# Another order of the pieces of a step in the five engines' queues of a Mamba and mixture-of-experts kernel

## What is computed

```
h = causal_conv(x_hat @ in_proj, 4 taps) + conv_b         # u
dt = clip(sigmoid(u @ dt_w.T + dt_b), 1e-4, 1);  Bm, Cm = u @ B_w.T, u @ C_w.T
state = exp(dt*A) * state + dt*Bm*u + 1e-6                # for each of 16 states, along 256 tokens
y = sum_n(state_n * Cm_n) + D*u;   x = x + (y * silu(z)) @ out_w.T
w = normalised top 2 of sigmoid(x_hat @ router_w.T + bias)
x = x + shared(x_hat) + sum_e w_e * (silu(x_hat @ wg_e.T) * (x_hat @ wu_e.T)) @ wd_e.T
```

## Time and profile before

| | |
|---|---|
| median of the runs | 1398.56 us (1398.08 to 1398.73) |
| the profiled execution: its span | 1397.1 us (its own time is this span and the launch around it, some 1.5 us by the median) |
| TensorE matmuls busy | 1212.7 us, 87% |
| VectorE busy | 1174.3 us, 84% |
| ScalarE busy | 916.8 us, 66% |
| GpSimd busy | 846.8 us, 61% |
| the chain that ended last | TensorE 35%, VectorE 31%, ScalarE 13%, issue 12%, GpSimd 5%, DMA 2% |
| mean granted TensorE clock | 0.981 of 2.4 GHz |

### The profile page before, as it was taken

How to read it: one execution, slowest core, us unless ns; L and a number is a source line. 1 busy time by engine, 2 the same in 40 slices (tenths; PEclk the granted TensorE clock), 3 DMA queues, 4 the chain that set the end, 5 groups by cost and what they waited for, 6 DMA issues and landing times.

```text
span 1397.1 us, 27129 instructions
## 1 busy us (share of the span) xinstructions
PE 1212.7 (87%) x8709; PEld 1013.2 (73%) x8709; DVE 1174.3 (84%) x2236; ACT 916.8 (66%) x1464; POOL 846.8 (61%) x1370
## 2 busy tenths in 40 slices
PE   6878897899989898998989899898989989898883
PEld 4556666577877777777777778777877878787773
DVE  1699999998898979998898989989798988998423
ACT  4665666577875766777676777668577768772321
POOL 4445445854366864768656783768647684665554
PEclk9899999999999999999999999999999999999997
DMA  6000000032322343143321433232330333256783
GB/s 179 1 1 9 1 9 6 22 125 61 114 82 64 106 136 103 44 128 99 121 67 34 147 97 98 86 111 81 109 120 29 125 92 121 78 184 190 251 271 85
DMA packets 111646, 132.29 MB, mean 95 GB/s; under 512 B 10128, under 2 KB 82704, under 8 KB 111504
## 3 DMA queue, kind: packets, MB, share of 16 engines
q1 hardware_dynamic: 98416, 111.31, 25.7%
q0 software_dynamic: 8192, 16.79, 4.0%
q10 hardware_dynamic: 4896, 2.43, 0.6%
HBM read 102.37 MB, written 28.11 MB: 93 GB/s over the span
## 4 chain that ended last, share of the span: by engine, by line
PE 35%; DVE 31%; ACT 13%; issue 12%; POOL 5%; DMA 2%; DVEq 0%; POOLq 0%; SPq 0%; ACTq 0%
DVE h L1281 14%; DVE yT L1299 11%; PE p_db L1036 5%; PE p_misc L1060 5%; PE p_hT L1053 5%; PE p_dn L1218 4%; PE p_gu L1206 3%; ACT dA L872 3%; ACT L969 2%; POOL ysel L791 2%; ACT hm L969 2%; PE p_gu L1197 2%; PE p_misc L1097 2%; PE p_misc L1141 1%; PE p_misc L1115 1%
## 5 line engine op out<-in xcount | busy, mean ns | idle before, releaser
L1281 DVE TENSOR_TENSOR_SCAN h<-dA,p_db 128x512 f32<-128x512 f32 x512 | 602.4, 1205 | 86.3 <-PE p_db L1036 85.3
L735 POOL TENSOR_SCALAR dBT<-wT,bcT 128x256 f32<-128x256 f32 x704 | 337.1, 479 | 249.2 <-ACT wT L903 140.1
L1299 DVE SCALAR_TENSOR_TENSOR yT<-p_hT,bcT,yT 128x256 f32<-128x256 f32 x960 | 402.2, 472 | 18.0 <-PE p_hT L1053 17.9
L872 ACT ACTIVATE dA<-dt_sb,A_sb 128x510 f32<-128x510 f32 x512 | 330.6, 710 | 26.6 <-DVE h L1281 25.5
L1036 PE MATMUL p_db<-ident,dBT 128*128 128x128 f32 x2048 | 284.4, 277 | 49.4 <-DVE h L1281 44.0
L1053 PE MATMUL p_hT<-ident,h 128*128 128x128 f32 x2048 | 288.9, 279 | 29.8 <-DVE yT L1299 16.6
L1036 PEld LDWEIGHTS p_db<-ident,dBT 128*128 128x128 f32 x2048 | 233.4, 142 | 96.7 <-issue 84.7
L1053 PEld LDWEIGHTS p_hT<-ident,h 128*128 128x128 f32 x2048 | 233.0, 143 | 74.8 <-issue 42.2
L777 POOL DMA_INDIRECT xs_dram<-xn,slot x128 | 127.0, 992 | 90.0 <-ACT dA L872 38.3
L929 ACT ACTIVATE dBT<-wT,eps,bcT 128x256 f32<-128x256 f32 x320 | 163.9, 593 | 0.0
L791 POOL DMA_INDIRECT ysel<-ys_dram,slot x128 | 123.5, 965 | 57.0 <-issue 33.9
(11 more groups left out here) (189 smaller groups left out, 1533.1 us busy)
## 6 DMA issues: line engine op xcount, KB each, us to landing
wring<-w_moe_dram SPq DMA_DIRECT2D x169, 384.0 KB, 4.3
xt<-xs_dram SPq DMA_DIRECT2D x41, 256.0 KB, 5.7
ys_dram<-yo SPq DMA_DIRECT2D x34, 256.0 KB, 2.3
dA<-w_moe_dram SPq DMA_DIRECT2D x16, 384.0 KB, 5.6
x_sb<-x_dram SPq DMA_DIRECT2D x16, 256.0 KB, 4.5
out_dram<-x SPq DMA_DIRECT2D x15, 256.0 KB, 2.5
xs_dram<-ysel SPq DMA_DIRECT2D x4, 512.0 KB, 6.0
xs_dram<-xn,slot POOLq DMA_INDIRECT x128, 2.3
```

The lines of the kernel that those rows point to most:

```text
L735: op = pool.tensor_scalar(dBT[:, j % DBT_RING, c], wT[:, g % 2, c], bcT[:, g % 2, c, n:n + 1], STATE_EPS, ALU.mult, ALU.add)
L872: act.activation(dst[:, :, 1:], src[:, :, 1:], ACT.Exp, scale=A_sb[:, half, n:n + 1]).then_inc(exp_done, 1)
L1281: dve.tensor_tensor_scan(h[:, j % 2, half], dA[:, j % DA_RING, half], p_db[half][:], 0.0, ALU.mult, ALU.add).then_inc(scan_done, 1)
L1299: op = dve.scalar_tensor_tensor(yT[:, g % 2, cc], p_hT[pair][:, c], bcT[:, g % 2, cc, NS + n:NS + n + 1], yT[:, g % 2, cc], ALU.mult, ALU.add)
```

## The change

In the last steps, of group 15's routing `r`: before `r0` to `r25` in a row after `lg`; after `lg r0-3 P P r4-12 P P r13-22 Q P P r23-25`. GpSimd: before `S S C S S C S...`, after `C C S S S S S...` (combs of group 11, scatters of the last batch, then gathers). The diff, cut to the tables spoken of:

```diff
 PE_SLOTS = (
-    "U h N G i0 i1 X", "h U yb0 N i0 i1 yb1 G", "X h U xnT i0 i1 N G", "h u0 N U v0 i0 i1 X X",
-    "N h U G op i0 i1", "U X G h u1 v1 G N i0 i1 h", "U X xn2T G i0 i1 dt0 f0 X",
-    "N h dt1 f1 N U i0 i1 logit X G", "h N U i0 i1 G bc N X", "h U i0 i1", "h G G N X U z0 i0 i1 z1",
-    "h X N U G i0 i1 X U rank", "N h i0 i1", "h G X wT0 U N wT1 G i0 i1 h X N X", "U G N i0 i1 h G",
-    "U i0 i1 X")
+    "X U i0 U N h N G i1", "h yb0 G i0 i1 h G N yb1", "i0 N i1 U U xnT h u0 i0", "G i1 v0 N X h op X U",
+    "i0 G X i1 h u1 v1 G X", "N U i0 i1 X U xn2T G h", "i0 dt0 N f0 i1 X N h i0", "dt1 f1 U i1 G logit h U X",
+    "i0 i1 X bc h X N i0 N", "i1 U h i0 G N z0 G X", "i1 h G U N i0 z1 G i1", "X U i0 h rank U N h i1",
+    "N wT0 X U G G wT1 i0 X", "N h i1 U i0 G i1 h X", "X U N i0 i1 G")
 DVE_SLOTS = (
-    "stats1 s0 s1 y0 P y1", "C Q s0 s1 Q P yd0 y0", "s0 s1 yd1 y1 Q C y0 y1", "s0 C C y0 s1 P y1 P Q",
-    "s0 s1 P y0 y1 x1 C", "stats2 s0 s1 C y0 Q Q P y1", "s0 s1 y0 P y1", "s0 y0 s1 C Q y1 s0 lg P Q",
-    "s1 Q C y0 P C", "s0 y1 s1 r y0 r y1 r P r r s0 r", "Q C s1 r y0 y1 r P r Q r s0 s1 r",
-    "r y0 r P y1 r C C Q r", "s0 r s1 r y0 y1 r r", "C P r r s0 s1 Q r y0 y1 r Q r",
-    "r r C s0 P s1 r r y0 r P y1", "s0 C s1 C Q y0 Q P y1")
+    "s0 stats1 P s1 y0 y1 C P s0 s1", "Q yd0 s0 s1 C y0 yd1 y1 Q C", "y0 y1 s0 s1 y0 P y1 P s0 Q",
+    "s1 y0 y1 Q Q x1 stats2 P s0 s1", "C y0 C y1 s0 P P s1 C Q", "y0 y1 s0 s1 C y0 y1 s0 P s1",
+    "Q lg Q y0 r y1 r P s0 r", "s1 Q r y0 y1 r P s0 r s1", "C Q r y0 C r y1 r Q s0", "r P C s1 r y0 r C y1 s0",
+    "r s1 r Q P C r C r y0", "r y1 r P r y0 r Q r s0", "s1 r y1 Q P r s0 r y0 r", "Q y1 r C s1 r s0 r P C",
+    "s1 y0 Q y1 C P r")
 ACT_SLOTS = (
-    "x x d x V m0 d E X", "m1 V x d", "X xnT d E V", "x E X V d", "u0 X x E E X u1 V x d", "V x E d X",
-    "xn2T V X", "E dt0 d dt1 x d V E x sig X", "X d E V", "d E bc x x V", "V z0 z1 E d x X",
-    "X E X V d d d x V", "E x wT0", "wT1 V X X", "x E V X d", "E X E V")
+    "V x d V x E", "d x m0 m1 d V", "X xnT X d E x", "u0 X x x X d", "d V E X x d", "d V E d u1 E", "V X x E xn2T V",
+    "X E E dt0 V d", "dt1 sig E X V x", "bc x X E X x", "V x z0 X E V", "V d z1 X E x", "d d E V d V",
+    "wT0 d d E wT1 x", "E x V x X X", "X V E X")
 POOL_SLOTS = (
-    "c", "c d d S d c c ln1 gate0 C C", "", "c d C c d gate1 C S S", "d C S c c S",
-    "C C ln2 d d d c c C c c S", "", "clip0 S d clip1 S C S d C d c c C S", "", "", "w0 w1 C S d c S", "C",
-    "", "d c S C d d S", "", "C C S S")
+    "c c C c C", "d S ln1 S d", "d S c gate0 gate1", "d C d c d", "S C c ln2 c", "c d S C S", "S C S C c",
+    "d d c S d", "C C S C S", "c S d c d", "clip0 clip1 c C c", "w0 C S w1 d", "c C C c d", "C d C S d", "S S")
...
 PE_FIRST = (
-    "xnT u0 v0", "u1 v1 dt0 f0", "dt1 f1 bc", "wT0 wT1", "h i0 i1 N G U X", "h i0 i1 N G U X",
-    "h i0 i1 N G U X", "h i0 i1 N G U X", "h i0 i1 N G U X", "h i0 i1 N G U X", "h i0 i1 N G U X",
-    "h i0 i1 N G U X", "h i0 i1 N G U X", "h i0 i1 N G U X", "h i0 i1 N G U X", "h i0 i1 N G U X",
...
+    "xnT u0 v0 u1 v1 dt0 dt1 f0 f1 i0 bc", "X h h i1 U i0 U wT0 G N h", "wT1 h G i1 G i0 X i1 N i0 X",
+    "i1 U X h N N X X U X i0", "U G h U G G i1 i0 N G N", "i1 X N i0 U i1 h h h i0 G", "i1 h i0 N U N i1 i0 i1 h G",
+    "U U U G i0 i1 i0 h X N X", "U i1 G N N G X i0 h h U", "i1 h i0 i1 i0 N G X z0 X i1", "N N G U U G N U z1 i0 X",
...
 ACT_FIRST = (
-    "xnT u0", "u1 dt0", "dt1 bc", "x x x x x x x x x x x x x", "wT0 wT1", "d", "d", "d", "d", "d", "d", "d",
-    "d", "d", "d", "d", "d", "d", "d", "x", "x", "x", "d", "d", "z0 z1", "V X E", "V X E", "V X E", "V X E",
...
+    "x xnT u0 x u1 x x x", "dt0 x d x dt1 x bc x", "x wT0 d wT1 x d x x", "x d d X d X d x", "d d V X d d z0 E",
+    "d E X V d X E E", "E d z1 V x X E E", "d V V E E X X V", "X V V V V E V X", "V X d X X E E X", "X E V E E V V V",
+    "E X")
...
 PE_LAST = (
-    "h yb0 yb1 X U op N", "N G X G U", "U G N xn2T X", "N logit U G X", "U N rank G X", "N U X G",
-    "N U G N X", "U G", "N X U G", "N X X G", "U G U U X", "N N X G", "N U G X", "X N U G", "N G U",
-    "N U G X X")
+    "h N U yb0 X", "U N G X X", "yb1 G G G op", "N U N xn2T X", "U U G logit X", "N U rank X G", "N N U X G",
+    "U N G U N", "U N G X G", "U X X G N", "X N U G X", "U G U X N", "N G X G U", "N X U X N", "G")
 DVE_LAST = (
-    "y0 y1 yd0 Q Q yd1 P P", "C s0 s1 C Q x1 stats2", "C P Q P", "lg C",
-    "r r r r r r r r r r r r r r r r r r r r r r r r r r Q r r P Q r C C", "", "Q C P Q Q P", "Q C", "P Q C",
-    "P C", "C P P Q Q P", "Q C", "Q P C", "P P Q C", "C", "C P")
+    "y0 C C Q C Q", "y1 yd0 s0 P P yd1", "P s1 x1 Q stats2 lg", "C r r r r P", "r r r r r r", "P r r r P r",
+    "r r r r r r", "r r Q r Q P", "r Q r Q r C", "P C P Q P r", "r C Q r C P", "C Q Q C P Q", "P C C C Q P",
+    "P Q C C Q P", "C Q")
 POOL_LAST = (
-    "", "gate0 S C C", "gate1", "S C ln2 C S S", "S C", "", "", "S S C C S S", "", "", "S C", "S C C C", "",
-    "S S C C C S", "", "S S C C")
+    "C C S", "C gate0 gate1", "C S ln2", "S C C", "C S S", "S S C", "C S C", "S C C", "S C S", "C S C", "S C S",
+    "S S")
...
@@ -1221,7 +1219,7 @@
                 if i == 1:
                     mm.then_inc(down_in_psum, 1)
 
-            begun = None
+            begun = set()
             for k in STEPS:
                 for name, u in in_turn((PE_FIRST, PE_SLOTS, PE_LAST), k):
                     if name == "h":
@@ -1232,10 +1230,9 @@
                         if name != "rank" or batch_of(k - 1) is not None:
                             use_misc(name, k + MISC_STAGE[name])
                     if name in MISC_REST.values():
-                        begun = name
+                        begun.add(name)
                     if name in MISC_REST:
-                        assert begun == MISC_REST[name]
-                        begun = None
+                        begun.remove(MISC_REST[name])
                     if name in MISC_REST and group_of(k, 1) is not None:
                         finish_misc(MISC_REST[name], k + 1)
                     if name == "X":
```

More of the change, by code:

```diff
@@ L107 @@
+    "c d S d c", "d c S d c", "S c")
 SP_FIRST = (
[3 rows of a table removed]
+    "T O W W T Y", "O O T W W O", "Y Y Y W W W", "T O T O T O", "O Y T Y T Y", "Y Y xl T O Y", "O Y W T O O",
+    "W O W T W T", "Y W W W Y T", "T T Y T Y W", "W O O Y O")
 PE_LAST = (
[L112 to L114 removed]
+    "h N U yb0 X", "U N G X X", "yb1 G G G op", "N U N xn2T X", "U U G logit X", "N U rank X G", "N N U X G",
@@ L115 @@
+    "U N G U N", "U N G X G", "U X X G N", "X N U G X", "U G U X N", "N G X G U", "N X U X N", "G")
 DVE_LAST = (
[3 rows of a table removed]
[3 rows of a table added]
 ACT_LAST = (
-    "E X V V Y E Y", "X", "V E X", "E E Y xn2T V sig X V Y", "X E V Y", "X E V", "Y Y X V V E", "E Y",
-    "X X E V", "X Y Y V E", "X E E Y", "X V E V Y", "X Y V", "V X E Y V", "E Y X", "Y X")
+    "X X V E X", "V E V E E", "xn2T X V Y sig", "Y X V Y V", "Y X E V E", "Y Y X E E", "Y V Y E E", "E Y V X V",
+    "X X X Y V", "E X V Y V", "Y E X Y X", "E Y V V E", "X Y E X Y", "V")
@@ L128 @@
+    "W O T", "W W O", "T W W", "O T W")
 MISC_STAGE = {"xnT": 1, "u0": 1, "u1": 1, "dt0": 1, "dt1": 1, "bc": 1, "z0": 1, "z1": 1,
```

11 lines of the change are left out of this document (4 added, 7 removed), and 11 rows, old and new, of tables (ACT_FIRST, DVE_FIRST, PE_FIRST, SP_FIRST).

## The result

The changed kernel takes 1331.12 us (median of four runs, 1329.77 to 1332.73) against 1398.64 for the kernel before beside it: a ratio of 0.951 (0.950 to 0.953), 67.5 us faster. The profiled execution spans 1328.0 us, before 1397.1: 69.1 less.

What follows compares the result with a forecast made beforehand. No single engine was taken as the bound: TensorE and VectorE wait for each other in heavy steps. Heavy steps -29.5 us (three quarters of 39.3), first steps and step 15 -6, end +4: 1398.6 - 31.5 = 1367, range 1350 to 1396.

Steps and rivals of the forecast that it cites:

- Part 2: The dt block (units 6 to 8): 2.2 us gained in an odd step, 0.9 more in an even one.
- Part 3: `wT` and the tail of a step: exponentials moved behind `wT1`, 0.2 us gained in an even step.
- Part 4: Head of a step, `i0(1)` hoisted: the place that costs, scan of unit 1 0.3 us later.
- The slower rival: Hoisted `i0` at each step's head idles TensorE 1.5 us, never given back: 1426, or 1410 with some gain; chance 0.15.
- the three quarters: Discount on the heavy steps' laid gain, because a laying leaves delays out: 39.3 us taken as 29.5.
- The laying: New TensorE and VectorE order laid over one odd and one even step: 2.7 and 4.3 us gained at VectorE.
- the end: Behind the last scan, slot to gathers: slot about 9.7 us later, gather 12 5.0 sooner; +4 us taken (+0 to +8).
- start: First steps: reordering around the scans of units 0 and 1 taken as 0 (-2 to +2); step 0 gains 2 us.
- step 15: The last of the steps 0 to 15: a gain of 1 us.
- the waits move: Rival, chance 0.18: each removed wait reappears at the next hand-over, a third of the gain left: 1387 (1382 to 1395).
- GpSimd at 0: GpSimd's new order, gathers and scatters ahead of clips, priced at 0, up to 1 us a step if `d` slips.
- parts 1 and 2: Convolution (0.5 us gained in odd, 3.2 in even steps) and dt block (2.2 in odd, 0.9 more in even).

Runs made afterwards that it cites:

- h3_from2: Kernel before with units 2 to 15 of each step in the new order, GpSimd and SP of the steps new, head and end old: 1332.9 us (0.953).
- h2_upto9: Kernel before with units 0 to 8 of each step in the new order, GpSimd and SP of the steps new, the rest old: 1370.1 us (0.980).
- e1_slots: Kernel before with only steps 0 to 15 in the new order on all five queues, first step and end old: 1324.2 us (0.947).
- e5_pool_last_new: Changed kernel with the old order behind step 15 on TensorE, VectorE, ScalarE and SP, the new one on GpSimd alone: 1324.1 us (0.947).

## Why the prediction was wrong in size and right in direction

**Part 2 was laid right.** From the start of `i0(5)` in an odd step the changed trace has `i(6)` at 6.49 (laid 6.5), `s0(6)` at 7.23 (7.1), `dt1` at 13.44 with no wait (13.5) and the end of `s1(8)` at 18.05 (18.2). **Part 3** too: `wT1` waits 0.3 us where 1.6 stood. **Part 4**: `i0(1)` waits 1.59 us (1.4 laid), and the scan of unit 1 starts 5.54 us into the step: no loss, where 0.3 was taken. By `h3_from2` the new head is even worth 8 us in the whole, though alone it gains nothing. The slower rival decides from 8.3 us on, and the step is far from it.

**First failed step: the three quarters.** "A laying by hand leaves delays out" took 9.8 us off a sum that was itself too small.

**Second: what was not laid.** The sum credited units 9 to 15 with 0.2 us in an even step. In the odd step before, VectorE waits 6.8 us in nine places; five of them are small (0.20, 0.22, 0.29, 0.28, 0.54) and one is 0.77 at unit 14. After, two are left, 1.37 and 0.56: 4.9 less, and the step is 4.8 shorter. The laying had 2.7. In an even step 9.2 us of waits became 3.0, and 1.0 us came from the small operations, 7.2 together (7.0 measured); the laying had 4.3, and "what follows there is VectorE's own work and keeps it" left out that this work itself depends on its order. That is 5 x 2.1 + 6 x 2.7 = 27 us, and the light steps gave 3.9 more than the 1 us each.

**Third: the end.** It was -4 and is -10.5. The way from slot to gather 12 is as forecast (10.6). `slot` is 14.0 us late where 9.7 was laid: `lg` comes 4.7 us later and not 2.1, and from `lg` to `slot` it is 9.3 longer and not 7.6. The gathers from 12 to 15 add 1.5, for which the sum had nothing. The granted clock, which the sum did not have at all, is 1 to 2 us of this: it is 0.67 and 0.65 in the two stretches of 5 us from 1226 on, and there an up of the shared expert takes 3.15 us for 1.97 and the transposes of `xn2T` 1.09 for 0.60.

9.8 + 27 + 3.9 + 1.5 (start) + 1.8 (step 15) less 6.5 (end) is 37.5, and the profiled executions differ by 37.6 from the forecast.

**The rival "the waits move"** is seen at the seam of `h2_upto9` (0.28 us before, 1.12 there) and nowhere in the whole order. **GpSimd at 0** was right as a sum and wrong as a reason: it was near 0 only because `ln2` was moved with TensorE's `xn2T`; with the whole old order of GpSimd the kernel loses 38 us, 23 of them for this piece (32 and 16 by the profiled executions). Nor is it quite 0: the operation of VectorE that GpSimd's product holds costs some 0.65 us in each even step, which the prediction did not have. **ScalarE**: 133 table loads, as forecast (59 + 40 + 16 + 16 + 2 for the three sets). Its old order under TensorE's new one was not tried: the queues would wait for each other in a circle. So ScalarE's own share stays open, as does what in the new units 9 to 15 brings the granted clock down at the end.

One figure of the prediction is off by itself: the slower rival with a third of parts 1 and 2 given back is 1426 - 12.7 = 1413, not 1410.

The fastest of the kernels are `e1_slots` and `e5_pool_last_new`, at 0.947 of the kernel before: the new steps with the old end (in the second but for GpSimd), 0.4% under the changed kernel by ratio.

## What to carry to other kernels

Where two engines hand work to each other all through a loop, lay the whole period of the new order, not only the places with the largest waits, and don't discount it: the step became as long as VectorE's own work plus the two waits that were left. What one stretch is worth alone says little of its worth in the whole (19 and 46 us here), since the next old hand-over can take back what the first half of a step gains; undoing it in the whole says it. And a piece that is moved earlier needs its producer moved too, even if that stands on the engine with the most slack: GpSimd's order alone gains nothing (23 to 30 us slower where it was run), and its absence from the new order costs 32 to 38.

## What the runs showed of the hardware that was not expected

On VectorE an operation on 64 elements takes some 0.25 us from its start to the next ahead of one that waits for its end, and 0.08 to 0.14 us ahead of one that doesn't. The Trainium skill (VectorE: DVE Perf Modes, The TRN2 errata) has a fixed cost for each instruction, exposed between instructions. The traces agree that there is one: rows are 0.2 us long for 64 elements and 0.69 for 512, from which some 0.07 us is an estimate for the 64 elements alone. But by them the time to the next start about halves when that one doesn't wait.

A small operation of VectorE on two inputs that begins while GpSimd multiplies two 128x512 tiles (`w`) is held: over all traces such operations took 0.45 to 1.29 us where they take 0.2 otherwise (two of 0.19 excepted), and the long ones ended some 0.1 us behind one of GpSimd's two instructions. Reductions, which have one input, took 0.18 to 0.20 us there. No term of the forecast's sum had it.

TensorE's granted clock was 0.52 (1.2 GHz for nearly all of 10 us) behind the same 3.1 us of idling in 8 that left it at 1.00 (2.4 GHz) in another kernel, and a projection of 16 matmuls then took 3.75 us for 2.02.
